# Side work behind every second block of keys on VectorE, ScalarE and GpSimd too, in the first attention

## The reference, cut to what matters

```
lat = layer_norm(latents);  ctx = layer_norm(context)
q = (lat @ Wq) -> (b, 16 heads, 512, 64)
k, v = split(ctx @ Wkv) -> (b, 16 heads, 1024, 64)
k = apply_rope(k, cos, sin)
attn = clip(q @ k.T * 64**-0.5, -11, 11)
attn = softmax(attn)
out = (attn @ v) -> (b, 512, 1024) @ Wo + bo
x = x + out
```

## Time and profile before

| | us |
|---|---|
| median of 3 runs | 2766.04 (2760.65 to 2767.31) |
| the profiled execution's own time | 2766.01 |
| its span, first to last instruction | 2764.3 |
| TensorE, VectorE, ScalarE, GpSimd busy | 2154.2, 1379.5, 757.4, 700.7 |

### The profile page before, as it was taken

The page is one execution under the profiler, slowest core; times in us unless marked ns, Lnnn a source line. Parts: engine busy times, 40 slices in busy tenths (PEclk is TensorE's granted clock), DMA queues, the critical chain, the costliest instruction groups (busy, mean ns, idle before and its releaser), DMA issues.

```text
span 2764.3 us, 34540 instructions
## 1 busy us (share of the span) xinstructions
PE 2154.2 (78%) x13832; PEld 1500.8 (54%) x13832; DVE 1379.5 (50%) x2156; ACT 757.4 (27%) x1164; POOL 700.7 (25%) x757
## 2 busy tenths in 40 slices
PE   2789898659958888885985787399678888469994
PEld 2445444248944444443883554299534544368883
DVE  4688888733136667675314543222465564412123
ACT  2444444212122333331112322000124445211111
POOL 3212121033320010001223221355411010154443
PEclk8899999869978999997996777599879999689997
DMA  4011000048920000001571000389300000078883
GB/s 142 16 30 32 23 26 18 8 158 284 316 98 8 11 15 10 8 8 41 182 254 37 16 12 5 118 311 328 131 12 18 10 11 3 22 267 294 294 293 103
DMA packets 96559, 274.66 MB, mean 99 GB/s; under 512 B 14128, under 2 KB 44592, under 8 KB 96016
## 3 DMA queue, kind: packets, MB, share of 16 engines
q0 software_dynamic: 45168, 206.99, 21.6%
q1 hardware_dynamic: 51232, 65.46, 7.6%
HBM read 239.50 MB, written 20.32 MB: 94 GB/s over the span
## 4 chain that ended last, share of the span: by engine, by line
PE 54%; DVE 20%; issue 10%; DMA 6%; ACT 5%; POOL 4%; another core or an unknown queue 0%; SPq 0%; DVEq 0%; POOLq 0%; ACTq 0%
PE psum L1976 11%; PE psum L277 9%; PE psum L1999 7%; PE psum L742 5%; PE psum L722 5%; DVE plain L888 5%; DVE plain L1513 3%; PE psum L1343 3%; PE psum L1316 2%; DMA plain<-sorted_x 2%; DMA plain<-in_l_en,plain 2%; PE psum L1360 2%; ACT plain L1028 2%; DVE plain L861 2%; PE psum L315 1%
## 5 line engine op out<-in xcount | busy, mean ns | idle before, releaser
L1976 PE MATMUL psum<-plain 128*128 128x128 f32 x3904 | 492.4, 279 | 10.4 <-DMA plain<-in_l_shared 8.6
L1976 PEld LDWEIGHTS psum<-plain 128*128 128x128 f32 x3904 | 484.8, 195 | 22.5 <-issue 9.7
L277 PE MATMUL psum<-split 128*128 128x256 f32 (+1 forms) x1728 | 379.9, 373 | 71.1 <-DVE split L350 9.8
L277 PEld LDWEIGHTS psum<-split 128*128 128x128 f32 x1728 | 286.8, 210 | 202.0 <-issue 115.9
L2100 POOL DMA_INDIRECT plain<-in_l_ffn,plain x274 | 259.9, 949 | 401.6 <-PE psum L1999 379.4
L1999 PE MATMUL psum<-plain 128*128 128x256 f32 x1160 | 303.8, 385 | 33.2 <-DVE plain L2065 30.6
L1028 ACT ACTIVATE plain<-psum 128x1024 f32<-128x1024 f32 x224 | 227.4, 1023 | 359.7 <-PE psum L742 246.1
L888 DVE TENSOR_TENSOR plain<-plain 128x1024 f32<-128x1024 f32 x200 | 265.6, 1328 | 12.4 <-ACT plain L1028 9.4
L722 PE MATMUL psum<-plain 128*64 128x512 f32 x896 | 241.8, 640 | 32.3 <-DVE plain L895 27.4
L742 PE MATMUL psum<-split 64*128 64x512 f32 x1536 | 237.0, 432 | 37.0 <-DVE plain L861 30.0
L1056 POOL TENSOR_TENSOR plain<-plain 128x512 f32<-128x512 f32 x48 | 67.7, 1410 | 673.1 <-DMA plain<-plain 669.9
(11 more groups left out here) (176 smaller groups left out, 2278.9 us busy)
## 6 DMA issues: line engine op xcount, KB each, us to landing
plain<-plain SPq DMA_DIRECT2D x192, 64.0 KB
plain<-sorted_x SPq DMA_DIRECT2D x76, 128.0 KB
sorted_y<-plain SPq DMA_DIRECT2D x76, 128.0 KB
plain<-in_l_w SPq DMA_DIRECT2D x20, 256.0 KB
plain<-in_l_ffn,plain POOLq DMA_INDIRECT x274
plain<-in_ctx SPq DMA_DIRECT2D x8, 512.0 KB, 5.9
plain<-in_l_wo SPq DMA_DIRECT2D x28, 128.0 KB, 2.0
plain<-in_l_tab SPq DMA_DIRECT2D x3, 1024.0 KB
```

The costliest lines, as they stand in the source:

```text
L277: m = t.e.matmul(out, lhs[x], rhs[y], start=(first and n == 0), stop=(last and n == 2), skip_group_check=skip)
L1976: m = t.e.matmul(K.bank(b)[:, 256 * z + P * f:256 * z + P * f + P], ws[:, f, c0:c0 + 128], xt[:, k, :], start=(f == 0 and k == 0 and z == ...
```

## The change

In the first attention (`own` is false) the table is made of four numbers, one for two blocks, and written as nothing behind the even block and all of it behind the odd one. The second attention keeps its table.

```diff
-            self.pace.append(paced(weights, total, [(kt + 1) / nk for kt in range(nk)]))
+            if own:
+                self.pace.append(paced(weights, total, [(kt + 1) / nk for kt in range(nk)]))
+            else:
+
+                two = paced(weights, total, [(kt + 2) / nk for kt in range(0, nk, 2)])
+                self.pace.append([x for n in two for x in (0, n)])
```

## The result

| | before | after |
|---|---|---|
| median, 22 runs each | 2764.88 us (2752.97 to 2776.17) | 2780.06 us (2763.90 to 2789.89) |
| ratio, 95% interval | | 1.0047 (1.0033 to 1.0062) |
| profiled execution, its span | 2766.01, 2764.3 us | 2774.52, 2772.7 us |

The changed kernel is slower by 0.47%, 13 us on 2765, with an interval from 9 to 17 us; the medians themselves differ by 15.2. The forecast was 2779 us, 0.46% more.

A forecast was written before the change was run, and what follows sets the result against it. The bound was taken as a chain passing between TensorE and VectorE, neither full. A loss of 1.25 less 0.4 gained, 0.85 us times 15 steps, gave 12.75 us, so 2766.0 + 12.8 = 2779 us; range 2760 to 2791.

The forecast's parts named there:

- VectorE's lateness sets the end of a step: At a step's end the division's matmul waits for VectorE's last add, after 1.08 us of idle TensorE.
- Clip 1 and the reciprocal: Start of the step: clip 1 now ahead of the reciprocal costs 0.15 us, bounds 0 and 0.69, and is absorbed.
- Add 1 meets GpSimd at its new place: First half: add 1, right behind clip 3, still takes 2.30 us beside GpSimd's first rope product, bounds 1.22 and 2.30.
- the 1.5 that would have spoken against the prediction: Sign against the forecast: exp 4 coming more than 1.5 us earlier against the division.
- The fourth output result waits: TensorE's fourth output result waits for the later output additions, so the next scores start 1.6 us late, bounds 0 and 1.74.
- The gain up to clip 7: First half of the step: 0.4 us gained, clip 7 at 224.9 instead of 225.34, bounds 0 and 1.55.
- The splits behind clip 7: End of the step: two splits behind clip 7 and add 5 delay the division's matmul by 1.25 us, bounds 0 and 1.3.
- The sum: First attention: 1.25 - 0.4 = 0.85 us lost a step, times 15 steps 12.75 us.
- the 28.4 to 28.6 that were named as its sign: Sign for the forecast: in a middle step the division's matmul comes 28.4 to 28.6 us after the one before.
- the third rival: Counted as slower, chance 0.15; against it, steps with 1.3 us idle pieces ran at full clock. Size not given.
- The total: Whole kernel: 2766.0 + 12.8 = 2779 us, 0.46% more, 2773 to 2785 by itself, chance 0.60.

The follow-up runs named there:

- The experiment with VectorE alone: Against the kernel before, only VectorE takes its side work behind every second block, ScalarE and GpSimd keep the old numbers: 37.2 to 37.4 us a plain step, 2911.8 us.
- with little GpSimd work: GpSimd's two rope instructions cover 64 of 512 columns in the first attention: 27.1 to 27.3 us a plain step on the changed kernel, 27.1 on the kernel before.
- blocks 4 to 7 alone: Against the kernel before, the change for blocks 4 to 7 only, on all three engines: 28.47 us in four plain steps, ratio 1.0080.
- the change with the output first: Against the changed kernel, VectorE does the four output additions ahead of add 1 behind block 3: 28.0 to 28.1 us in five plain steps, ratio 1.0032 to the kernel before.
- the version that won: Against the kernel before, blocks 0 to 5 changed, 6 and 7 as before, output additions ahead of add 1: 27.1 us in five plain steps, ratio 0.9975, median 2756.51 us.
- the version with the splits ahead of add 5: Against the changed kernel, VectorE does the key and query splits ahead of add 5 behind clip 7: one plain step 28.31 us, others 29.3 to 32.6, 2793.5 us.

## Why the prediction was right

- **VectorE's lateness sets the end of a step.** Right: TensorE waits for the last add in 13 steps after the change.
- **Clip 1 and the reciprocal.** 0.15 us said and taken as absorbed, so that it is not in the sum; 0.09 measured. The experiment with VectorE alone shows that this rests on ScalarE's move.
- **Add 1 meets GpSimd at its new place.** Right: 2.29 us against the 2.30 taken, with GpSimd's first product at 444.21, 0.34 us before the add. The rule that I quoted from the Trainium skill, SBUF — State Buffer, "Who interferes with whom", agrees: the pairs of rows alternate, and with little GpSimd work the slow adds are gone. The rule as quoted is on instructions with two inputs; the rows show that clips, with one, are held as well. In four steps add 1 took 1.22 us, and exp 4 came 2 us or more earlier against the division, more than the 1.5 that would have spoken against the prediction; but the two plain middle ones among them lasted 28.2 and 28.4 us, no less than the others.
- **The fourth output result waits.** Right: a new wait of 1.32 us. Scores 4 start 9.75 us after the reciprocal (447.86 - 438.11), against 8.27 in the earlier trace rows: 1.5 us late, 1.6 said.
- **The gain up to clip 7.** 0.4 us said, 0.50 measured from division to division as the prediction counts (0.59 from the reciprocal, less the 0.09 above), by the path that was described: exp 4 released by scores and early by 1.0 us (1.0 said; 1.12 from the reciprocal), clip 4 held by GpSimd's fourth instruction (1.32 us for a clip that takes 0.69).
- **The splits behind clip 7.** 1.25 us said, 1.07 measured; the scores' wait for them (1.30 us, said 1.5) is in front of the last add, and 0.78 us of idle TensorE still follows it (1.0 said).
- **The sum.** 0.85 us a step said, 0.73 measured on plain steps. A plain step lasts 28.2 us, just below the 28.4 to 28.6 that were named as its sign, in part because the step that the prediction started from was itself 0.16 us longer than the usual one. 12.75 us for the attention said, 9.9 in the pair of profiles. Step by step the difference runs from -0.8 to +2.3 us, so the total is less exact than it looks: the first two steps in the sum lost 2.3 and 1.5 us, while three steps with weight splits, at a granted clock of 0.96, 0.92 and 0.94 before and 1.00 after, changed by +0.2, +0.4 and -0.8. The granted clock of the stretch rose from 0.98 to 0.99, so the third rival went the other way, as its last sentence allowed. What it feared did happen in two other versions with the new tail (blocks 4 to 7 alone, and the change with the output first): two plain steps of each ran at 0.95 or 0.96 and were 0.7 to 1.2 us longer than their neighbours.
- **The total.** 2779 us said, 2780.06 measured. That these lie within 1 us is luck in part: the sum was too large by 2.9 us against the profiles, and the interval of the ratio is 8 us wide.
- **What I did not see.** I checked TensorE's pace for exp 6 but not for exp 7, where the query copy stood ahead of it with no slack. It did not matter for this change, which moves that copy behind exp 7, and it mattered in every partial version that I then expected to gain.

## What to carry to other kernels

When an order is changed on several engines, walk one step of each of them for every partial version too: here each half alone, and each engine alone, cost more than the whole. Look in front of each instruction on the chain for the second condition that is met just before the first; where two meet within 0.3 us, taking one away gains little, 0.4 us here. Try work that other engines wait for (the first read of a ring of banks) ahead of work that only its own engine needs soon: four additions moved ahead of one were worth 1.57 us of a 28.65 us step with the old tail, and 0.2 with the new one. And read more than one step: the longer ones at a lower clock, and the shorter ones where a collision did not happen, told as much as the typical one.

## What the runs showed that I had not expected

Two VectorE instructions with both inputs in SBUF can each be held by GpSimd in turn: in the version that won, add 1 took 1.49 us beside GpSimd's second instruction and add 2 took 2.31 beside its fourth. And in the version with the splits ahead of add 5, TensorE's idle pieces of 1.30 and 0.78 us became one of 2.03, and the mean granted clock over the attention was 0.94 instead of 0.99, in one run.
